# A last low-rank product in two fp32r passes, with high and low parts packed along the contraction

## The reference, cut to what matters

```
flat   = layernorm(y)                                # 448 x 512
logits = flat @ Wr.T                                 # 4 experts
gates  = softmax over the 2 largest logits           # zero for the other experts
mid    = einsum('tf,erf->ter', flat, A)              # 4 experts x rank 16
delta  = sum_e gates[t,e] * (mid[t,e] @ B[e].T) * SCALE
out    = y + tanh(g_ffn) * delta
```

## Time and profile before

| | |
|---|---|
| median of 3 runs | 2008.38 us (2006.62 to 2009.34) |
| span of the profiled execution | 2005.4 us (its own time is not given) |
| instructions | 32965 |
| PE busy | 1976.7 us, 99% of the span |
| DVE, ACT, POOL busy | 1235.0, 1034.3, 311.6 us |

### The profile page before, as it was taken

The page is one execution under the profiler, slowest core; times in us unless marked ns, Lnnn a source line. Parts: engine busy times, 40 slices in busy tenths (PEclk is TensorE's granted clock), DMA queues, the critical chain, the costliest instruction groups (busy, mean ns, idle before and its releaser), DMA issues. The chain is left out here.

```text
span 2005.4 us, 32965 instructions
## 1 busy us (share of the span) xinstructions
PE 1976.7 (99%) x12404; PEld 1775.9 (89%) x12404; DVE 1235.0 (62%) x2639; ACT 1034.3 (52%) x1754; POOL 311.6 (16%) x227
## 2 busy tenths in 40 slices
PE   7999999999999999999999999999999999999998
PEld 7989889988899988998899988998899998999786
DVE  6766556666666666666666666666665666566544
ACT  6655555554545555555644555455554555455532
POOL 5511111111111111111111111111111111111200
PEclk9999999999999999999999999999999999999998
DMA  7611212111211212221111112221111112121270
GB/s 227 248 56 35 35 18 44 35 31 20 43 10 33 36 17 44 35 35 20 39 19 25 35 20 41 36 35 20 39 25 26 28 20 41 36 33 15 48 263 19
DMA packets 74904, 94.41 MB, mean 47 GB/s; under 512 B 22692, under 2 KB 49444, under 8 KB 74760
## 3 DMA queue, kind: packets, MB, share of 16 engines
q1 hardware_dynamic: 73752, 86.01, 20.4%
q10 hardware_dynamic: 1008, 6.42, 0.8%
HBM read 76.64 MB, written 15.77 MB: 46 GB/s over the span
## 5 line engine op out<-in xcount | busy, mean ns | idle before, releaser
L673 POOL TENSOR_TENSOR k_lo<-k_work,k_hi 128x500 fp32r<-128x500 f32 x192 | 244.1, 1285 | 1541.0 <-ACT k_hi L720 1513.3
L821 PE MATMUL low_banks<-wv_hi,cT_hi 128*125 128x256 f32 x1536 | 443.1, 288 | 0.0
L821 PE MATMUL low_banks<-wv_hi,cT_lo 128*125 128x256 f32 x1536 | 431.0, 281 | 0.0
L821 PE MATMUL low_banks<-wv_lo,cT_hi 128*125 128x256 f32 x1536 | 430.9, 281 | 0.0
L1027 DVE TENSOR_TENSOR pT<-t_banks,pT 125x448 fp32r<-125x448 f32 x384 | 236.0, 622 | 242.8 <-ACT pT L785 242.8
L1002 DVE CUSTOM_DVE_ANT_0 prob<-low_banks,mask_t 112x500 f32<-112x500 f32 x384 | 259.1, 678 | 178.2 <-PE low_banks L845 176.9
L785 ACT ACTIVATE pT<-t_banks 125x448 fp32r<-125x448 f32 x384 | 205.1, 543 | 309.2 <-PE t_banks L857 308.2
L760 ACT ACTIVATE prob<-prob,neg_max 112x1500 f32<-112x1500 f32 x128 | 198.6, 1552 | 289.7 <-DVE neg_max L1007 288.9
L805 PE MATMUL low_banks<-cT_hi,wk_hi 128*128 128x500 f32 x768 | 312.0, 406 | 0.0
L805 PE MATMUL low_banks<-cT_hi,wk_lo 128*128 128x500 f32 x768 | 298.6, 389 | 0.0
L805 PE MATMUL low_banks<-cT_lo,wk_hi 128*128 128x500 f32 x768 | 298.3, 388 | 0.0
(11 more groups left out here) (136 smaller groups left out, 2910.2 us busy)
## 6 DMA issues: line engine op xcount, KB each, us to landing
stage<-in_ctx_dram SPq DMA_DIRECT2D x72, 250.0 KB
attn_by_head<-attn SPq DMA_DIRECT2D x65, 112.0 KB, 1.7
wq_raw<-in_L_xattn_wq_dram SPq DMA_DIRECT2D x7, 1024.0 KB, 7.2
q_raw<-q_by_head SPq DMA_DIRECT2D x64, 112.0 KB, 4.9
inv_b<-inv_by_head SPq DMA_DIRECT2D x64, 112.0 KB, 5.1
head_rows<-in_ctx_dram SPq DMA_DIRECT2D x24, 250.0 KB
mask_t<-in_mask_BxSxS_ff_dram SPq DMA_DIRECT2D x16, 328.1 KB
stage<-in_L_xattn_wo_dram SPq DMA_DIRECT2D x4, 1024.0 KB, 7.3
```

Of the source, the lines that this page charges most:

```text
L673: nc.gpsimd.tensor_tensor(k[1][:, c * SC:(c + 1) * SC], k_rot[:, s], f32(k[0][:, c * SC:(c + 1) * SC]), ALU.subtract).then_inc(k_lo, 1)
L821: mm = nc.tensor.matmul(sv_banks[0:ST, m % 2, t * PAIR:(t + 1) * PAIR], cT[a][:, d, tile * ST:(tile + 1) * ST], w[1][mv][:, d, g * DH:g * ...
```

## The change

The operands of the last product get a high and a low part, stacked along the contraction. `bT` becomes two tiles of fp32r: the high part of B twice over (128 rows), and the low part (64 rows). `midT` becomes one tile of 128 rows: the high part of mid in the upper half and the low part in the lower. A first product over 128 rows gives (mid_hi + mid_lo) @ B_hi, a second over 64 rows adds mid_hi @ B_lo. For this `b_raw` is doubled by POOL before it is turned, `mid` is written twice by DVE, the high parts are written by ACT, and DVE's two copies become subtractions that wait for ACT.

```diff
-    bT = sb("bT", [ER, D])
+    b_twice = sb("b_twice", [P, DC, 2, ER])
+    bT = [sb(f"bT_{n}", [2 * ER, D], F32R) for n in ("hi", "lo")]
-    mid = sb("mid", [ROWS, NTT, EXPERTS, RANK])
-    midT = sb("midT", [ER, TOK])
+    mid = sb("mid", [ROWS, NTT, 2, EXPERTS, RANK])
+    midT = sb("midT", [2 * ER, TOK], F32R)
...
@@ gpsimd, behind the mask of earlier experts
+        pool.wait_ge(small_loaded, SMALL)
+        for u in range(2):
+            nc.gpsimd.tensor_copy(b_twice[:, :, u], b_raw[:, :, :, :].rearrange("p c e r -> p c (e r)")).then_inc(b_doubled, 1)
...
@@ scalar, between the four turned copies and tanh; and at its end
+        act.wait_ge(small_banked, 2)
+        nc.scalar.activation(bT[0][:, :], yT_banks[0:2 * ER, 1, :], ACT.Copy).then_inc(bT_hi, 1)
...
+        act.wait_ge(midT_banked, 1)
+        nc.scalar.activation(midT[:, :], yT_banks[0:2 * ER, 0, 0:TOK], ACT.Copy).then_inc(midT_hi, 1)
...
@@ tensor
+        pe.wait_ge(b_doubled, 2)
-            mm = nc.tensor.transpose(yT_banks[0:ER, 1, c * P:(c + 1) * P], b_raw[:, c].rearrange("p e r -> p (e r)"), ident[:, :])
+            mm = nc.tensor.transpose(yT_banks[0:2 * ER, 1, c * P:(c + 1) * P], b_twice[:, c].rearrange("p t n -> p (t n)"), ident[:, :])
...
-        pe.wait_ge(mid_ready, 1)
+        pe.wait_ge(mid_ready, 2)
-            mm = nc.tensor.transpose(yT_banks[0:ER, 0, t * ROWS:(t + 1) * ROWS], mid[:, t].rearrange("p e r -> p (e r)"), ident[0:ROWS, 0:ROWS])
+            mm = nc.tensor.transpose(yT_banks[0:2 * ER, 0, t * ROWS:(t + 1) * ROWS], mid[:, t].rearrange("p u e r -> p (u e r)"), ident[0:ROWS, 0:ROWS])
...
-            nc.tensor.matmul(acc[0:ROWS, t, :], midT[:, t * ROWS:(t + 1) * ROWS], bT[:, :], start=True, stop=True).then_inc(delta_ready, 1)
+            rows = slice(t * ROWS, (t + 1) * ROWS)
+            nc.tensor.matmul(acc[0:ROWS, t, :], midT[:, rows], bT[0][:, :], start=True, stop=False)
+            nc.tensor.matmul(acc[0:ROWS, t, :], midT[0:ER, rows], bT[1][0:ER, :], start=False, stop=True).then_inc(delta_ready, 1)
...
@@ vector
-        dve.wait_ge(small_banked, 2)
-        nc.vector.tensor_copy(bT[:, :], yT_banks[0:ER, 1, :]).then_inc(small_copied, 1)
+        dve.wait_ge(bT_hi, 1)
+        nc.vector.tensor_tensor(bT[1][0:ER, :], yT_banks[0:ER, 1, :], f32(bT[0][0:ER, :]), ALU.subtract).then_inc(small_copied, 1)
...
-        nc.vector.tensor_tensor(mid[:, :, :, :], z[:, :, 0:ER].rearrange("p t (e r) -> p t e r", e=EXPERTS),
-                                gates[:, :, :, None].broadcast_to([ROWS, NTT, EXPERTS, RANK]), ALU.mult).then_inc(mid_ready, 1)
-        dve.wait_ge(midT_banked, 1)
-        nc.vector.tensor_copy(midT[:, :], yT_banks[0:ER, 0, 0:TOK]).then_inc(midT_ready, 1)
+        for u in range(2):
+            nc.vector.tensor_tensor(mid[:, :, u], z[:, :, 0:ER].rearrange("p t (e r) -> p t e r", e=EXPERTS),
+                                    gates[:, :, :, None].broadcast_to([ROWS, NTT, EXPERTS, RANK]), ALU.mult).then_inc(mid_ready, 1)
+        dve.wait_ge(midT_hi, 1)
+        nc.vector.tensor_tensor(midT[ER:2 * ER, :], yT_banks[ER:2 * ER, 0, 0:TOK], f32(midT[ER:2 * ER, :]),
+                                ALU.subtract).then_inc(midT_ready, 1)
```

More of the change, by code:

```diff
@@ L1155, in output_part @@
     gate_steps, earlier_steps, exp_ready, mid_ready = sem("gate_steps"), sem("earlier_steps"), sem("exp_ready"), sem("mid_ready")
+    b_doubled, bT_hi, midT_hi = sem("b_doubled"), sem("bT_hi_ready"), sem("midT_hi_ready")
     midT_banked, midT_ready, delta_ready, res_ready, stored = (
```

## The result

The changed kernel takes 2010.95 us in the median of 20 runs (2008.41 to 2013.50), the kernel before 2008.26 us (20 runs, 2006.05 to 2010.01). The ratio is 1.0014, with a 95% interval of 1.0007 to 1.0020: 2.7 us slower. This is outside the range on record by 0.45 us, though within 0.2% of no change.

A forecast was written before the change was run, and what follows sets the result against it. TensorE was taken to bound the kernel until 1990.0 us, then a dependent string across engines. +2.05 us for the earlier operands and -2.40 at the end gave -0.35: median 2008.0 us, range 2006.4 to 2010.5.

The forecast's parts named there:

- The hole: PE's wait before L1090 for bT's later subtraction: 1.83 us plus 0.22 for a slow first product, +2.05 us.
- The covers: POOL's b_raw copies, the b transposes, tanh and its table load, before the last products: hidden or free, put at nothing.
- no table is loaded before midT's copy: Rival in the end string: ACT reloads a table before midT's copy, +1.28 us, 2009.3; chance 0.05 shared with late stores.
- The string's small terms: End string before the products: second mid product +0.35, transposes with 128 columns +0.05, ACT copy ahead of DVE's subtraction +0.57 us.
- The stores: Four output stores at the end, 0.85 us apart in place of 1.7, were said to fit: +0.1 us.
- The rival by which stores come no faster than 1.7 us apart: Output stores at the end become the bound, the last late by 2.55 us, 2010.5; chance 0.05 shared with a table load.
- The products: L1290 at the end: eight fp32r products take 3.71 us against 7.18 for four plain ones, -3.47 us.
- The rival by which an fp32r product costs half a plain one: At L1290 nothing is gained from the new products: +3.1 us in all, 2011.5; chance 0.03.
- The clock behind the hole: Rival: PE's wait before L1090 brings 3.4 us at half clock, 1.7 us lost, +1.35 in all, 2009.7; chance 0.30.
- The full clock at the end: Rival: last products at full clock take 2.07 us and transposes half, -2.5 us in all, 2005.9; chance 0.03.
- part 2: The dependent string at the end, from the second mid product to the output stores: forecast sum -2.40 us.

The follow-up runs named there:

- the 128-row product alone: The changed kernel with B's low part subtracted for both halves and the second product over 128 rows instead of 64: 2008.05 us, ratio 1.0003.
- both repairs: The changed kernel with ACT's high-part copy of bT ahead of its turned copies and the second product over 128 rows: 2005.13 us, ratio 0.9989.
- the hole alone: The kernel before plus an unused ACT copy of the turned B, which DVE's bT copy waits for; products stay plain fp32: 2010.38 us, ratio 1.0017.
- the grouped one: The changed kernel with the same eight last products reordered, the four over 128 rows first, then the four over 64: 2011.36 us, one execution.
- PE kept busy: The kernel with both repairs plus 14 unread PE products while DVE forms the gates and 4 behind mid's transposes: 2003.95 us, ratio 0.9983.

## Why the prediction was wrong

**The hole: right.** 2.05 us was forecast for the wait and the restart, 1.91 + 0.23 = 2.14 came. The path was the one described: the last turned copy on ACT, the high part, the subtraction, PE. Putting the one copy ahead removes it.

**The covers: right.** POOL's copies of b_raw take 0.40 us each and start by 1930.9, 30 us ahead of PE; the b transposes take 0.44 us as before; tanh and the table load are off the chain; no table is loaded before midT's copy.

**The string's small terms: right.** The second mid +0.33 (forecast 0.35), the transposes +0.05 (0.05), ACT in front of DVE +0.58 (0.57).

**The stores: too small, but hidden here.** The span ends 2.66 us after the last res, 2.64 before; but in the changed kernel the res start 1.39 us apart, not the 0.85 of the forecast. In the two kernels that do reach 0.85, with the 128-row product alone and with both repairs, the span ends 2.9 and 3.1 us after the last res, and a store takes longer from issue to landing than the 2.2 us of the earlier trace rows; with both repairs:

```profile
out_dram<-res SPq DMA_DIRECT2D x4, 224.0 KB, 2.6
```

So the term is nearer 0.3 to 0.45 than 0.1. The rival by which stores come no faster than 1.7 us apart, +2.55, is ruled out by the same two spans.

**The products: wrong.** This is the step that failed, in the sentence "contraction over 64 or 128 rows makes no difference here: the rows differ in columns only". The price of 0.425 us was read from a stream in which all neighbours stand on 128 rows; in the changed kernel they alternate, each load stands in the open, and the eight take 5.65 us: -1.53 in place of -3.47. The rival by which an fp32r product costs half a plain one (7.18 / 8 = 0.90 us) was not it either; 0.70 lies between. Corrected by this term alone the sum is -0.35 + 1.94 = +1.6, which is what the profiled execution shows. With equal heights the forecast of 3.71 us is met (3.77), and with both repairs the string nearly so: -2.43, where the terms without the stores' 0.1 add up to -2.50.

**The clock behind the hole: half right.** The mechanism and the price were given (3.4 us at half, 1.7 us lost; 1.57 measured), and that it then comes back. The argument for 0.30, that the hole at 1.83 us is shorter than the 2.19 us in the earlier trace rows, was weak. That longer hole, 2.2 us in front of L845, stands in all nine traces, and in each the granted clock falls behind it (a mean of 0.50 to 0.85 from 1888 to 1891 us). And three of the four profiled executions with the hole (the one with the hole alone, the 128-row one and the grouped one, each with 4.56 or 4.57 us for the first twelve products) lost it, and of the 20 timed ones about half by the mean clock. By the same reading it is four of eleven with the hole alone and three of ten with the 128-row product, so how often the clock goes is not known well. 1.6 us with the loss in half of the executions gives between 1.6 and 3.3 in the median; 2.7 was measured. What decides in a given execution whether the clock goes was not tried. It took both misses to leave the range: by the sum, the products alone give 2010.0, the lost clock alone 2009.7, and both 2011.7.

**The full clock at the end: its price was too high.** The rival put part 2 at -4.5 from PE's times alone. With PE kept busy the clock was full, but then DVE's four res set the end: z to the end of the last res takes 8.84 us, 3.9 less than the 12.73 before, and the span ends 3.3 us after it instead of 2.64.

**What stays open.** That a change of height exposes the weight load is shown; why is not. The Trainium skill (TensorE: Matmul & The Clock Gate, section "Step-by-step: what each phase is for") says that PE pulls a weight load ahead of running matmuls where the row groups don't conflict or the load goes to the background buffer. The equal-height rows agree with the second case (the load at 2000.71 runs under the product that starts at 2000.70, on the same 128 rows), and by that rule a load in the open would be one that neither case covers; no run here shows which part of the rule a change of height breaks.

## What to carry to other kernels

When a producer is split into a high and a low part, look at where the new copy stands in its engine's queue, and who waits for the last of the two: a copy that was 4 us early became a hole of 1.9 us in TensorE's stream. A matmul's price, taken from another line of the trace, holds only if its neighbours are alike: here eight products cost 3.8 us at one height and 5.65 at two, and padding the short ones to full height was free. A dependent string at the end is worth a look at the granted clock: idle time in front of the last products doubled their price, and products that nobody reads gave it back.

## What the runs showed of the hardware that was not expected

Alternating 128 and 64 rows of contraction shows the weight load of every fp32r product (112 stationary columns, 512 moving ones): 0.70 us apart against 0.43 at a granted clock of 0.50, and 0.41 against 0.23 at 1.00. A hole of 1.9 us in an otherwise full TensorE stream was followed, in three of four profiled executions, by 3.4 us at half clock.
